# Two expert biases and a projection bias, moved from GpSimd to TensorE in the last layer of a four-layer kernel

## The chip, the cores and the metric

The kernel is one program on one core of a Trainium2 chip. The metric is the device time of one execution in microseconds. The engines are TensorE (PE; PEld is its weight load), VectorE (DVE), ScalarE (ACT), GpSimd (POOL) and SyncE (SP, which issues the transfers). The program of each engine is written out by hand, with semaphores between them.

## The reference

Four layers, each of the form x = x + attention(norm(x)) + ffn(norm(x)), on x of 8 batches, 512 tokens and 128 dimensions, all in f32. Only layer 3 is touched by the change:

```python
def _L3_attn_ref(x, Wq, bq, Wk, bk, Wv, bv, Wp, bp, bias_table, temperature):
    ...            # 16 heads of 8 dimensions, no causal mask, bias by distance
    att = jax.nn.softmax(energy / (scaling * temp), axis=-1)
    out = jnp.einsum('bhqk,bhkd->bhqd', att, v)
    out = out.transpose(0, 2, 1, 3).reshape(B, N, C)
    return out @ Wp + bp

def _L3_ffn_ref(x, Wr, br, W1, b1, W2, b2):
    k = 2
    scores0 = x[:, 0, :] @ Wr + br
    _, idx = jax.lax.top_k(scores0, k)            # two experts for each batch
    W1g, b1g = (W1[idx], b1[idx])
    W2g, b2g = (W2[idx], b2[idx])
    h = jnp.einsum('bsd,bkde->bkse', x, W1g) + b1g[:, :, None, :]
    h = jax.nn.gelu(h, approximate=False)
    o = jnp.einsum('bkse,bkef->bksf', h, W2g) + b2g[:, :, None, :]
    return jnp.sum(o, axis=1) / k
```

So a batch of layer 3 adds the same row of 128 numbers, (b2[e0] + b2[e1]) / 2 + bp, to each of its 512 tokens.

## The kernel before

x stays in SBUF for the whole program as [128, 32, 128] (token in a tile, tile, dimension); a batch is NT = 4 tiles. Layer 3 runs over the eight batches in a loop of pairs, with the last pair written out behind the loop. The heads of a batch are handled in four groups of four. Each group is first gone through for the row maxima ("max": PE's L501 with bias rows L505 to L510, DVE's L525), the maxima are turned into extra rows of Q (DVE L533 to L537, PE L550, DVE L558, a transfer at L483), and then gone through again for the exponentials ("score": PE's L572 with L576 and L579, ACT's L594) and the product with V ("attend": PE's L609, copied by DVE at L617). A list of steps fixes the order; each engine walks the same list and does its share of each step. While a group is in "score", the next group is in "max".

Beside the attention steps of the first group of a batch's successor, with six steps between one and the next, stands the tail of the batch: "hidden" (PE L2273, ACT L2243), "turn" (the division of the last group: PE L623, DVE L629 and L630), "mix" (PE L2281, DVE L2335), "turn_att" (PE L638, ACT L643) and "out" (PE L2289, DVE L2343). In the last batch the tail stands alone at the end. The start of the next batch ("center": DVE L359, L363, then POOL L387 and L389 for rstd, then DVE L371; "norm": PE L395; "k", "q", "v": PE L414 and L411; "choice": PE L2266, DVE L2322 to L2328) stands beside the scores of its predecessor's second group.

The steps of the tail share PSUM bank 1 in turns: `take` waits until the turn before has been emptied, `ready` until a named turn has been emptied, `there` until it has been filled. "aT" is the turn right before "out", and "h1" comes before "mix". "mix" multiplies the hidden values of the two experts by their second weights; DVE then makes acc = bank / 2 + x. "out" multiplies the turned attention by Wp; DVE writes x = bank + acc.

SP fetches the chosen experts' w1, w2, b1 and b2 in `pick`, eight transfers a batch, for the next batch once the last turn of the current one ("out") is filled. Before the change b2 lies in DRAM repeated 128 times, so that each of its transfers brings [128, 128], and bp is loaded once with a broadcast over the partitions. POOL's program for a batch is: rstd, the splitting of Q (L438 to L443), and then the bias work of L2223 to L2233, for which it waits for the experts. Four instructions make the constant row and add it to the batch's x in place. DVE waits for the count `bias_in` in "mix".

Two places in layers before it are of use for comparison: L2062 in layer 2 is a matmul with 32 rows of contraction, L2073 one with 64 columns of weights, and L2081 and L2083 alternate between 128 and 65 rows of contraction.

Of the kernel before, what the change touches and what calls it, by code (L numbers as in the profile page):

```python
# [7 lines left out]
ALU = mybir.AluOpType  # L8
# [127 lines left out]
def build(nc, a, out, layers=(0, 1, 2, 3)):  # L136

    stack = ExitStack()
    with stack:
# [211 lines left out]
        def settle(eng):  # L351


            eng.sem_inc(passed, 1)
# [477 lines left out]
        def load(sp, L, dst, src):  # L832
            sp.dma_start(dst, src).then_inc(L.weights, 16)
            L.loads += 1

        def pe_logits(pe, L, b, w, e):
            take(pe, L, b, "logit")
# [1302 lines left out]
        def layer3():  # L2140
# [8 lines left out]
            L.hankel = L.probs[:, 0:H * HANKEL // T, :].rearrange("p a (c i) -> p (a c) i", i=HANKEL)  # L2149
            L.table = carve([H, 384])  # L2150
            L.last = carve([H, 1])
            L.bp = carve([P, D])
            L.const = carve([P, D])
            L.wr, L.br = carve([P, E3]), carve([P, E3])
            L.sc, L.top, L.idx = carve([P, E3]), carve([P, 8]), carve([P, 8], U32)
            L.w1, L.w2 = carve([P, TOP3, D]), carve([P, TOP3, D])
            L.b1 = [carve([P, 1]) for _ in range(TOP3)]
            L.b2 = [carve([P, D]) for _ in range(TOP3)]
            L.hT = carve([P, TOP3, T])
            L.acc = carve([P, NT, D])  # L2160
            L.tabled = nc.dram_tensor("bias_by_distance", [H, 384], F32, kind="Internal").ap()
            L.chain = s("dve_chain", 19)
            L.chosen = s("experts_chosen", 1)
            L.picked = s("experts_in", 16 * 4 * TOP3, 1)
            L.bias_in = s("bias_added", 4)
            L.started += [L.picked]
            L.table_dve, L.table_dma = sem("table_dve"), sem("table_dma")
            L.bias_full, L.bias_free = sem("bias_full"), sem("bias_free")
# [13 lines left out]
            def sp_prog(sp):  # L2182
                L.loads = 0
                load(sp, L, L.table[:, 0:TABLE3], a["L3_attn_bias_table"])
                load(sp, L, L.scale, a["L3_attn_temperature"].partition_broadcast(P))
                for dst, name in ((L.w["k"], "L3_attn_Wk"), (L.w["q"], "L3_attn_Wq"), (L.w["v"], "L3_attn_Wv"),
                                  (L.w["o"], "L3_attn_Wp"), (L.bq, "L3_attn_bq"), (L.bk, "L3_attn_bk"),
                                  (L.wr, "L3_ffn_Wr")):
                    load(sp, L, dst, a[name])
                load(sp, L, L.bp, a["L3_attn_bp"].partition_broadcast(P))  # L2190
                load(sp, L, L.bv, a["L3_attn_bv"].partition_broadcast(P))
                load(sp, L, L.br, a["L3_ffn_br"].partition_broadcast(P))
                sp.wait_ge(L.table_dve, 3)
                sp.dma_start(L.tabled, L.table[:]).then_inc(L.table_dma, 16)
                sp.wait_ge(L.table_dma, 16)

                sp.dma_start(L.hankel[:], bass.AP(L.tabled.tensor, 0, [[1, P], [384, H], [1, HANKEL]])
                             ).then_inc(L.table_dma, 16)

                def pick(b):  # L2200
                    sp.wait_ge(L.late.full.sem, L.late.full.at(b, 0))
                    settle(sp)
                    sp.wait_ge(L.chosen.sem, L.chosen.at(b, 1))
                    settle(sp)
                    for k in range(TOP3):
                        e = sp.value_load(L.idx[0:1, k:k + 1], min_val=0, max_val=E3 - 1)
                        for dst, src in ((L.w1[:, k, :], a["L3_ffn_W1"][bass.ds(e, 1), :, :]),
                                         (L.w2[:, k, :], a["L3_ffn_W2"][bass.ds(e, 1), :, :]),
                                         (L.b1[k], a["L3_ffn_b1"][bass.ds(e, 1), :, :]),
                                         (L.b2[k], a["L3_ffn_b2"][bass.ds(e, 1), :, :])):  # L2210
                            sp.dma_start(dst, src.rearrange("e p c -> (e p) c")).then_inc(L.picked.sem, 16)
                sp_expand_ahead(sp, L, pick)

            def pool_prog(pool):
                pool_attention_setup(pool, L)

                def body(b):
                    pool_norm(pool, L, b)
                    pool_split_q(pool, L, b)
                    c = L.bias_in  # L2220
                    pool.wait_ge(L.picked.sem, L.picked.at(b, 16 * 4 * TOP3))
                    settle(pool)
                    pool.tensor_tensor(L.const[:], L.b2[0][:], L.b2[1][:], ALU.add).then_inc(c.sem, 1)  # L2223
                    pool.wait_ge(c.sem, c.at(b, 1))
                    settle(pool)
                    pool.tensor_scalar(L.const[:], L.const[:], 1.0 / TOP3, None, ALU.mult).then_inc(c.sem, 1)
                    pool.wait_ge(c.sem, c.at(b, 2))
                    settle(pool)
                    pool.tensor_tensor(L.const[:], L.const[:], L.bp[:], ALU.add).then_inc(c.sem, 1)
                    pool.wait_ge(c.sem, c.at(b, 3))  # L2230
                    settle(pool)
                    rows = x[:, bass.ds(b.index * NT, NT), :]
                    pool.tensor_tensor(rows, rows, L.const[:].unsqueeze(1).to_broadcast([P, NT, D]),  # L2233
                                       ALU.add).then_inc(c.sem, 1)
                each_batch(pool, body)

            def act_prog(act):
# [13 lines left out]
            def pe_prog(pe):  # L2251
                pe.wait_ge(L.weights, NW)
                pe.wait_ge(L.setup, 3 * L.copies)
                pe.wait_ge(L.padded, L.copies)

                pe.wait_ge(L.table_dma, 32)
                for n in range(H // 2):
                    if n >= 1:
                        pe.wait_ge(L.bias_free, n)
                    pe.matmul(bank[1][:], flip[:], L.hankel[:, 2 * n:2 * n + 2, :].rearrange("p h i -> p (h i)"),  # L2260
                              start=True, stop=True).then_inc(L.bias_full, 1)
                pe.wait_ge(L.bias_free, H // 2)

                def choice(pe, L, b, _):
                    bk = take(pe, L, b, "score")
                    fill(L, "score", pe.matmul(bk[:, 0:E3], xnT[b.parity][:, 0:1].to_broadcast([P, P]), L.wr[:],  # L2266
                                               start=True, stop=True))

                def hidden(pe, L, b, _):
                    pe.wait_ge(L.picked.sem, L.picked.at(b, 16 * 4 * TOP3))  # L2270
                    for k in range(TOP3):
                        bk = take(pe, L, b, f"h{k}")
                        fill(L, f"h{k}", pe.matmul(bk[:], L.w1[:, k, :], xnT[b.parity][:], start=True, stop=True))  # L2273

                def mix(pe, L, b, _):
                    take(pe, L, b, "mix")
                    ready(pe, L, b, f"h{TOP3 - 1}")
                    for t in range(NT):
                        cols = slice(t * P, (t + 1) * P)
                        for k in range(TOP3):  # L2280
                            ins = pe.matmul(bank[1][:, cols], L.hT[:, k, cols], L.w2[:, k, :], start=(k == 0),  # L2281
                                            stop=(k == TOP3 - 1))
                    fill(L, "mix", ins)

                def finish(pe, L, b, _):
                    take(pe, L, b, "out")
                    ready(pe, L, b, "aT")
                    for t in range(NT):
                        ins = pe.matmul(bank[1][:, t * P:(t + 1) * P], L.attT[:, t * P:(t + 1) * P], L.w["o"][:],  # L2289
                                        start=True, stop=True)  # L2290
                    fill(L, "out", ins)
                L.own_pe = {"choice": choice, "hidden": hidden, "mix": mix, "out": finish}

                def trip(b, more):
                    take_steps(pe_step, pe, L, b, more_steps if more else last_steps)
                pipelined(pe, L, lambda b: take_steps(pe_step, pe, L, b, first_steps), trip)

            def dve_prog(dve):
# [31 lines left out]
                def mix(dve, L, b, _):  # L2330
                    rows = x[:, bass.ds(b.index * NT, NT), :]
                    bk = there(dve, L, b, "mix")
                    dve.wait_ge(L.bias_in.sem, L.bias_in.at(b, 4))
                    settle(dve)
                    emptied(L, "mix", dve.scalar_tensor_tensor(  # L2335
                        out=L.acc[:], in0=bk[:].rearrange("p (t n) -> p t n", t=NT), scalar=1.0 / TOP3,
                        in1=rows, op0=ALU.mult, op1=ALU.add))
# [83 lines left out]
def _layouts(v):  # L2421
# [44 lines left out]
    out["L2_ffn_ba_up"] = v["L2_ffn_ba_up"].reshape(E2, 1, D)  # L2466
    for name in ("L3_attn_Wq", "L3_attn_Wk", "L3_attn_Wv", "L3_attn_Wp", "L3_ffn_Wr", "L3_ffn_W1", "L3_ffn_W2"):
        out[name] = by_dim(v[name]) if name in ("L3_attn_Wq", "L3_attn_Wk") else v[name]
    out["L3_attn_bp"] = v["L3_attn_bp"]
    out["L3_attn_bias_table"] = c(v["L3_attn_bias_table"].T)  # L2470
    out["L3_ffn_b1"] = v["L3_ffn_b1"].reshape(E3, D, 1)
    out["L3_ffn_b2"] = np.broadcast_to(v["L3_ffn_b2"][:, None, :], (E3, P, D))

    p, f = np.arange(P)[:, None], np.arange(P)[None, :]
    out["const_ident"] = np.eye(P, dtype=np.float32)
# [21 lines left out]
```

## Time and profile before

| what | value |
|---|---|
| median of three runs | 3440.54 us (3432.38 to 3443.14) |
| the profiled execution | 3443.14 us, span 3441.3 us |
| PE / PEld / DVE / ACT / POOL busy | 2630.3 / 1659.2 / 1621.3 / 1217.4 / 596.5 us |
| mean granted clock of TensorE | 0.874 of full |
| instructions on POOL | 600 |

The busy times are of the whole span. TensorE's busy time counts the modelled time of each matmul from start to end, which overlaps with that of the next; how long a matmul holds the engine is seen from the start of the next one. "Idle before" names, in brackets behind a row, how long the engine stood before this instruction and what it then went on for.

### The profile page before, as it was taken

What the parts mean: (1) busy time and instruction counts of PE and PEld (TensorE: products, weight loads), DVE (VectorE), ACT (ScalarE), POOL (GpSimd) and SP (SyncE); (2) the same over time, 40 slices, a digit from 0 to 9 for tenths busy, and PEclk for the clock granted to TensorE, in tenths of its full rate; (3) what the DMA queues carried; (4) which work ended last, traced back from release to release, by engine and by line L of the source; (5) the groups of instructions that cost most, each with busy time, mean ns of one, the idle gap of its engine ahead of it and who ended that gap; (6) DMA issues with size and microseconds to landing.
All of it is one profiled execution on the core that took longest, in us unless ns stands there. A gap on an engine that the chain in (4) does not pass through costs nothing. (4 is left out here: it accounts for less than half of the span.)

```text
span 3441.3 us, 52452 instructions
## 1 busy us (share of the span) xinstructions
PE 2630.3 (76%) x16466; PEld 1659.2 (48%) x16466; DVE 1621.3 (47%) x4013; ACT 1217.4 (35%) x2249; POOL 596.5 (17%) x600
## 2 busy tenths in 40 slices
PE   3677777799883778888887577777855888888887
PEld 1344444488771556656676244433423444444443
DVE  4556566400001444444433566666634555555563
ACT  0333333344433222222122244444421544444454
POOL 3322223000004433333102211111011000000000
PEclk7888889899995777778898699998977999999998
DMA  3111211266661000000054121111101111110111
GB/s 101 56 52 59 67 61 58 76 194 199 190 172 52 23 16 15 17 16 13 8 176 135 49 57 53 50 45 42 40 30 45 40 38 43 43 37 21 34 38 30
DMA packets 117031, 214.47 MB, mean 62 GB/s; under 512 B 20984, under 2 KB 89632, under 8 KB 109856
## 3 DMA queue, kind: packets, MB, share of 16 engines
q1 hardware_dynamic: 105088, 188.97, 18.3%
q0 software_dynamic: 10240, 20.99, 2.1%
q8 instruction: 143, 2.34, 0.3%
q10 hardware_dynamic: 1440, 1.18, 0.1%
q14 instruction: 120, 0.98, 0.1%
HBM read 158.50 MB, written 51.40 MB: 61 GB/s over the span
## 5 line engine op out<-in xcount | busy, mean ns | idle before, releaser
L525 DVE TENSOR_REDUCE arena<-bank 128x1 f32<-128x512 f32 (+3 forms) x1216 | 757.8, 658 | 207.2 <-PE bank L507 81.1
L501 PE MATMUL bank<-arena 125*128 125x512 bf16 (+3 forms) x1536 | 479.2, 349 | 165.9 <-DVE arena L525 91.8
L594 ACT ACTIVATE arena<-bank 128x512 f32<-128x512 f32 x640 | 370.5, 596 | 576.5 <-PE bank L584 563.2
L572 PE MATMUL bank<-arena 128*128 128x512 bf16 (+3 forms) x1536 | 461.3, 344 | 37.4 <-DMA arena<-arena 28.6
L594 ACT ACTIVATE arena<-bank,arena 128x512 f32<-128x512 f32 x512 | 339.3, 687 | 368.3 <-PE bank L572 208.5
L501 PEld LDWEIGHTS bank<-arena 125*128 125x128 bf16 x1536 | 143.6, 102 | 414.6 <-DVE arena L525 242.1
L609 PE MATMUL bank<-arena 128*32 128x512 f32 (+3 forms) x3072 | 329.9, 526 | 10.8 <-issue 6.3
L572 PEld LDWEIGHTS bank<-arena 128*128 128x128 bf16 x1536 | 140.1, 102 | 265.2 <-issue 139.7
L617 DVE COPY arena<-bank 128x512 f32<-128x512 f32 x96 | 66.4, 691 | 413.8 <-PE bank L609 398.3
L1854 DVE TENSOR_TENSOR arena<-bank,arena 128x512 f32<-128x512 f32 (+3 forms) x256 | 109.6, 482 | 199.5 <-PE bank L1720 193.7
L1098 PE MATMUL bank<-arena 128*128 128x128 f32 x1664 | 202.6, 275 | 0.1
L1245 ACT ACTIVATE arena<-bank,arena 128x256 f32<-128x256 f32 x320 | 131.9, 470 | 196.2 <-PE bank L1295 196.2
L1738 PEld LDWEIGHTS bank<-arena 128*128 128x128 f32 x1280 | 185.8, 232 | 22.3 <-issue 19.5
L1098 PEld LDWEIGHTS bank<-arena 128*128 128x128 f32 x1664 | 194.0, 192 | 0.5 <-ACT arena L1245 0.4
L1020 POOL DMA_INDIRECT back_rows<-sorted_out,back_now x160 | 154.0, 963 | 217.5 <-issue 155.1
L1738 PE MATMUL bank<-arena 128*128 128x65 f32 x1280 | 189.9, 316 | 1.0 <-DVE arena L1867 1.0
L1295 PE MATMUL bank<-arena 128*128 128x256 f32 x640 | 158.7, 391 | 38.1 <-DMA arena<-in_L_ffn_w 37.6
L1379 DVE TENSOR_TENSOR arena<-bank,arena 128x256 f32<-128x256 f32 x80 | 33.9, 424 | 322.4 <-PE bank L1098 322.4
L515 PE MATMUL bank<-mask_q,identb 128*128 128x128 bf16 (+2 forms) x704 | 183.5, 261 | 0.0
L1206 POOL DMA_INDIRECT sorted_in<-xn,arena x128 | 123.9, 968 | 333.4 <-PE bank L584 313.5
L584 PE MATMUL bank<-mask_k,identb 128*128 128x256 bf16 (+1 forms) x640 | 170.6, 267 | 0.0
L1720 PE MATMUL bank<-arena 64*128 64x128 f32 (+3 forms) x512 | 113.5, 554 | 55.3 <-DVE arena L1854 52.2
(249 smaller groups left out, 3702.5 us busy)
## 6 DMA issues: line engine op xcount, KB each, us to landing
arena<-in_L_ffn_w SPq DMA_DIRECT2D x80, 578.0 KB, 4.0
arena<-k_parts SPq DMA_DIRECT2D x48, 576.0 KB
arena<-q_parts SPq DMA_DIRECT2D x48, 576.0 KB
arena<-in_L_ffn_w SPq DMA_DIRECT2D x24, 768.0 KB, 4.5
arena<-sorted_in SPq DMA_DIRECT2D x104, 128.0 KB, 2.4
sorted_out<-arena SPq DMA_DIRECT2D x104, 128.0 KB, 4.0
k_parts<-arena SPq DMA_DIRECT2D x24, 384.0 KB
q_parts<-arena SPq DMA_DIRECT2D x72, 128.0 KB
```

What stands on the lines that cost most here:

```text
L501: ins = pe.matmul(mx[:, k * w:(k + 1) * w], Qx[0:KMAX, h, q * P:(q + 1) * P], Kx[0:KMAX, h, 0:w], start=(k == 0 or not L.causal), stop=not ...
L515: ins = pe.matmul(edge, identb[:], mask_q[:].unsqueeze(1).to_broadcast([P, n_heads, P]), start=False, stop=True, skip_group_check=True)
L525: dve.reduce_max(L.mx[:, g % 2, q, heads[0]:heads[-1] + 1], mx[:, 0:w * len(heads)].rearrange("p (j k) -> p j k", k=w), AX.X).then_inc(L.m ...
L572: ins = pe.matmul(st[:, c:c + w], Kx[:, h, kb * P:(kb + 1) * P], Qx[:, h, T - w:T], start=(c == 0), stop=not (L.causal or far), skip_group ...
L584: ins = pe.matmul(edge, identb[:], mask_k[:].unsqueeze(1).to_broadcast([P, len(at), P]), start=False, stop=True, skip_group_check=True)
L594: act.activation(L.probs[:, n % L.PR, 0:w], st[:, 0:w], ACT.Exp, scale=L.scale).then_inc(L.st_free.sem, 1)
L609: ins = pe.matmul(bank[2][j * VW:(j + 1) * VW, T - w:T], copy_of(L.Vx, b)[:, kb, g * HG + j, :], L.probs[:, (n + i) % L.PR, c:c + w], star ...
L1020: pool.indirect_dma_start(back_rows[:, t, k, :], None, L.ys, bass.IndirectOffsetOnAxis(L.back_now[b.parity][:, r:r + 1], 0)).then_inc(L.go ...
L1098: ins = pe.matmul(bank[2 + j % 2][:, h * D:(h + 1) * D], L.hT[j % 2][:, f, h * P:(h + 1) * P], down(j, f), start=(f == 0), stop=(f == 3))
L1245: act.activation(L.hT[j % 2][:, c, :], bank[4 + n % 4][:, c % 2 * BLK:(c % 2 + 1) * BLK], ACT.Gelu, bias=L.wbuf[j % 3][:, L.B1 + c:L.B1 + ...
L1295: ins = pe.matmul(bank[4 + n % 4][:, c % 2 * BLK:(c % 2 + 1) * BLK], L.wbuf[j % 3][:, L.W1 + c * P:L.W1 + (c + 1) * P], L.xT[j % 2][:], st ...
L1738: ins = pe.matmul(bk[:, t * V1W:(t + 1) * V1W], L.am[:, SLOTS * (h % 4) + slot, c:c + P], L.V[b.parity][:, kb, h, :], start=(kb == 0), sto ...
```

## The change

The constant row is no longer made and added by POOL. Instead PE adds the biases in PSUM: a matmul whose weights are one row of ones, [1, 128], and whose moving operand is the bias as one row adds the bias to all 128 tokens of a tile. `pe_bias` does this for a whole bank of four tiles at once, with the bias repeated four times by its access pattern (1 row by 512 columns). In "mix", the first expert's b2 is brought in this way, and the second's by four matmuls of 1 row by 128 columns, one ahead of each tile's two full matmuls. In "out", bp is brought in by `pe_bias` ahead of `pe_out`, which is a helper that the other layers use already. b2 and bp become [1, 128] in SBUF and are no longer repeated in DRAM. DVE's wait for `bias_in` in "mix" goes, as do the four POOL instructions of each batch.

```diff
+        def pe_bias(pe, bias):
+
+            return pe.matmul(bank[1][:], ones[0:1, :],
+                             bias[0:1, :].rearrange("p (o n) -> p o n", o=1).to_broadcast([1, NT, D]),
+                             start=True, stop=False, skip_group_check=True)
...
-            L.bp = carve([P, D])
-            L.const = carve([P, D])
+            L.bp = carve([1, D])
...
-            L.b2 = [carve([P, D]) for _ in range(TOP3)]
+            L.b2 = [carve([1, D]) for _ in range(TOP3)]
...
-            L.bias_in = s("bias_added", 4)
...
-                                  (L.wr, "L3_ffn_Wr")):
+                                  (L.bp, "L3_attn_bp"), (L.wr, "L3_ffn_Wr")):
                     load(sp, L, dst, a[name])
-                load(sp, L, L.bp, a["L3_attn_bp"].partition_broadcast(P))
...
                     pool_norm(pool, L, b)
                     pool_split_q(pool, L, b)
-                    c = L.bias_in
-                    pool.wait_ge(L.picked.sem, L.picked.at(b, 16 * 4 * TOP3))
-                    settle(pool)
-                    pool.tensor_tensor(L.const[:], L.b2[0][:], L.b2[1][:], ALU.add).then_inc(c.sem, 1)
...
-                    pool.tensor_scalar(L.const[:], L.const[:], 1.0 / TOP3, None, ALU.mult).then_inc(c.sem, 1)
...
-                    pool.tensor_tensor(L.const[:], L.const[:], L.bp[:], ALU.add).then_inc(c.sem, 1)
...
-                    pool.tensor_tensor(rows, rows, L.const[:].unsqueeze(1).to_broadcast([P, NT, D]),
-                                       ALU.add).then_inc(c.sem, 1)
...
                     take(pe, L, b, "mix")
                     ready(pe, L, b, f"h{TOP3 - 1}")
+                    pe_bias(pe, L.b2[0])
                     for t in range(NT):
                         cols = slice(t * P, (t + 1) * P)
+                        pe.matmul(bank[1][:, cols], ones[0:1, :], L.b2[1][:], start=False, stop=False,
+                                  skip_group_check=True)
                         for k in range(TOP3):
-                            ins = pe.matmul(bank[1][:, cols], L.hT[:, k, cols], L.w2[:, k, :], start=(k == 0),
-                                            stop=(k == TOP3 - 1))
+                            ins = pe.matmul(bank[1][:, cols], L.hT[:, k, cols], L.w2[:, k, :], start=False,
+                                            stop=(k == TOP3 - 1), skip_group_check=True)
...
                     take(pe, L, b, "out")
-                    ready(pe, L, b, "aT")
-                    for t in range(NT):
-                        ins = pe.matmul(bank[1][:, t * P:(t + 1) * P], L.attT[:, t * P:(t + 1) * P], L.w["o"][:],
-                                        start=True, stop=True)
-                    fill(L, "out", ins)
+                    pe_bias(pe, L.bp)
+                    fill(L, "out", pe_out(pe, L, b))
...
                     bk = there(dve, L, b, "mix")
-                    dve.wait_ge(L.bias_in.sem, L.bias_in.at(b, 4))
-                    settle(dve)
...
-    out["L3_ffn_b2"] = np.broadcast_to(v["L3_ffn_b2"][:, None, :], (E3, P, D))
+    out["L3_ffn_b2"] = v["L3_ffn_b2"].reshape(E3, 1, D)
```

## Rows read from the trace of the kernel before

**Rows 1.** Page, part 1: busy time, share, instructions; the row of PE.
```profile
PE 2630.3 (76%) x16466; PEld 1659.2 (48%) x16466; DVE 1621.3 (47%) x4013; ACT 1217.4 (35%) x2249; POOL 596.5 (17%) x600
```
**Rows 2.** Windows: span, then busy of PE, PEld, DVE, ACT, POOL, clock, DMA.
```profile
2732.00:2837.00 105.00, 87.83 (x516) 49.61 (x515) 59.65 (x123) 50.33 (x75) 6.91 (x9) 0.96 0.12 35
...
3362.00:3441.00 79.00, 59.63 (x336) 29.72 (x328) 29.27 (x56) 34.93 (x52) 2.68 (x4) 0.89 0.10 27
```
**Rows 3.** Timeline around "mix" of one batch: start us, length us, instruction.
```profile
2736.96 1.95 PE L2281 MATMUL bank<-arena 128*128 128x128 f32 x16
...
2738.74 0.38 PE L501 MATMUL bank<-arena 125*128 125x512 bf16 x1
...
2738.96 0.38 PE L572 MATMUL bank<-arena 128*128 128x512 bf16 x1
...
2739.26 0.69 DVE L2335 SCALAR_TENSOR_TENSOR arena<-bank,x 128x512 f32<-128x512 f32 x1 [1.61 <-PE bank L2281]
...
2740.61 0.39 PE L501 MATMUL bank<-arena 125*128 125x512 bf16 x1 [0.83 <-DVE arena L525]
```
**Rows 4.** Timeline around "out" of the same batch.
```profile
2744.79 1.06 PE L2289 MATMUL bank<-arena 128*128 128x128 f32 x8
...
2745.69 0.38 PE L501 MATMUL bank<-arena 125*128 125x512 bf16 x1
...
2745.89 0.69 DVE L2343 TENSOR_TENSOR x<-bank,arena 128x512 f32 x1 [0.72 <-PE bank L2289]
...
2748.31 0.33 PE L550 MATMUL bank<-identb,arena 128*12 128x128 bf16 x3 [1.80 <-DVE arena L537]
```
**Rows 5.** Timeline in layer 2: into 32 rows and out again.
```profile
2317.75 0.22 PE L515 MATMUL bank<-mask_q,identb 128*128 128x128 bf16 x1
...
2317.90 1.13 PE L2062 MATMUL bank<-arena 32*128 32x512 f32 x4
...
2318.96 0.39 PE L501 MATMUL bank<-arena 125*128 125x512 bf16 x1
```
**Rows 6.** Timeline in layer 2: 65 rows, first and last of four.
```profile
2339.60 0.39 PE L2083 MATMUL bank<-arena 65*128 65x128 f32 x2
...
2340.94 0.39 PE L2083 MATMUL bank<-arena 65*128 65x128 f32 x2
```
**Rows 7.** Timeline in layer 2: 64 columns of weights and what follows.
```profile
2332.20 1.07 PE L2073 MATMUL bank<-xnT,arena 128*64 128x512 f32 x2
...
2333.21 0.39 PE L501 MATMUL bank<-arena 125*128 125x256 bf16 x2
```
**Rows 8.** Timeline in layer 3: one full f32 matmul and what follows.
```profile
2765.11 1.02 PE L414 MATMUL bank<-xnT,arena 128*128 128x512 f32 x2
...
2765.97 0.38 PE L501 MATMUL bank<-arena 125*128 125x512 bf16 x1
```
**Rows 9.** Timeline behind rows 4: 12 columns beside 32 columns.
```profile
2748.43 0.63 PE L609 MATMUL bank<-arena 128*32 128x512 f32 x3
2748.48 0.22 PE L550 MATMUL bank<-identb,arena 128*12 128x128 bf16 x1
```
**Rows 10.** Timeline at the norm of two batches, POOL and DVE.
```profile
2755.61 1.27 POOL L2233 TENSOR_TENSOR x<-x,arena 128x512 f32 x1 [0.29 <-POOL arena L2229]
...
2756.96 0.23 POOL L387 TENSOR_SCALAR rstd<-mean_var 128x4 f32<-128x4 f32 x1
...
2758.51 1.11 DVE L371 TENSOR_SCALAR xn<-x,mean_var,rstd 128x128 f32 x4 [2.02 <-POOL rstd L389]
...
2861.20 0.23 POOL L387 TENSOR_SCALAR rstd<-mean_var 128x4 f32<-128x4 f32 x1 [2.54 <-DVE mean_var L363]
```
**Rows 11.** Timeline of the tail of the last batch.
```profile
3425.22 2.05 PE L2281 MATMUL bank<-arena 128*128 128x128 f32 x16 [0.68 <-DVE arena L630]
...
3427.46 0.69 DVE L2335 SCALAR_TENSOR_TENSOR arena<-bank,x 128x512 f32<-128x512 f32 x1 [2.30 <-PE bank L2281]
...
3429.63 1.74 PE L2289 MATMUL bank<-arena 128*128 128x128 f32 x8 [0.77 <-ACT arena L643]
```

More of the change, by code:

```diff
@@ L2219, in body @@
                     pool_split_q(pool, L, b)
-                    c = L.bias_in
-                    pool.wait_ge(L.picked.sem, L.picked.at(b, 16 * 4 * TOP3))
-                    settle(pool)
-                    pool.tensor_tensor(L.const[:], L.b2[0][:], L.b2[1][:], ALU.add).then_inc(c.sem, 1)
-                    pool.wait_ge(c.sem, c.at(b, 1))
-                    settle(pool)
-                    pool.tensor_scalar(L.const[:], L.const[:], 1.0 / TOP3, None, ALU.mult).then_inc(c.sem, 1)
-                    pool.wait_ge(c.sem, c.at(b, 2))
-                    settle(pool)
-                    pool.tensor_tensor(L.const[:], L.const[:], L.bp[:], ALU.add).then_inc(c.sem, 1)
-                    pool.wait_ge(c.sem, c.at(b, 3))
-                    settle(pool)
-                    rows = x[:, bass.ds(b.index * NT, NT), :]
-                    pool.tensor_tensor(rows, rows, L.const[:].unsqueeze(1).to_broadcast([P, NT, D]),
-                                       ALU.add).then_inc(c.sem, 1)
                 each_batch(pool, body)
@@ L2468, in _layouts @@
         out[name] = by_dim(v[name]) if name in ("L3_attn_Wq", "L3_attn_Wk") else v[name]
-    out["L3_attn_bp"] = v["L3_attn_bp"]
+    out["L3_attn_bp"] = v["L3_attn_bp"].reshape(1, D)
     out["L3_attn_bias_table"] = c(v["L3_attn_bias_table"].T)
     out["L3_ffn_b1"] = v["L3_ffn_b1"].reshape(E3, D, 1)
-    out["L3_ffn_b2"] = np.broadcast_to(v["L3_ffn_b2"][:, None, :], (E3, P, D))
+    out["L3_ffn_b2"] = v["L3_ffn_b2"].reshape(E3, 1, D)
     p, f = np.arange(P)[:, None], np.arange(P)[None, :]
```

## The prediction

> **What bounds the kernel now.** I read the page first: PE is the busiest engine of the whole span [rows 1]. The change touches layer 3 alone (the last quarter of the span), so I then read the stretches of one batch each. In one of 105 us, PE is busy 87.83 us, DVE 59.65, ACT 50.33 and POOL 6.91; the last stretch, where nothing runs ahead for a next batch, looks alike [rows 2]. The reader is to see that POOL has a hundred microseconds of room in a batch and PE very little. Third, the timeline around the two places that the change makes longer on PE. At "mix", PE goes straight from its 16 records to the next L501, DVE stands waiting 1.61 us for "mix" and starts L2335 behind it, and a later L501 of PE waits in turn for DVE [rows 3]. At "out", PE goes straight on to L501, DVE waits 0.72 us for the result, and PE later waits 1.80 us at L550 for the chain on DVE that began behind it [rows 4]. So each of the two sits on a path PE, DVE, PE without slack: what is added there moves everything behind it. Last, the timeline at the norm of the following batch, where POOL's rstd is awaited by DVE, and PE behind DVE [rows 10].
>
> **What the change adds on PE, per batch.** An f32 matmul appears as two records.
> 1. Two bias matmuls with 512 columns (one in "mix", one in "out"). The nearest row is L414, full shape: its two records start at 2765.11 and the next matmul at 2765.97, so 0.86 us [rows 8]. Twice that is 1.72 us.
> 2. Four matmuls of one row by 128 columns with the second expert's bias. In "mix" eight matmuls of 128 columns hold PE from 2736.96 to 2738.74, 0.22 us each [rows 3]. Four are 0.89 us.
> That a matmul of one row costs as much as one of 128 is taken from L2083: 65 rows alternate with 128 rows, and four alternations are spaced (2340.94 - 2339.60) / 3 = 0.447 us a pair, 0.223 us a matmul, the same 0.22 [rows 6]. Together 2.61 us a batch, 20.9 us over eight.
> 3. What a change of the array's shape costs. With 65 rows there is none [rows 6]. With 32 rows there is: L515 with 128 bf16 columns starts at 2317.75 and L2062 only 0.15 us later, where 128 columns take some 0.05 (a quarter of the 0.22 us by which bf16 matmuls of 512 columns follow one another in the timeline, as from 2738.74 on), so about 0.10 us to enter. Its four records, equal in time to one full 0.86 us, hold the next L501 back until 2318.96, 1.06 us, so 0.20 us to leave [rows 5]. L2073 with 64 columns holds the next L501 back for 2333.21 - 2332.20 = 1.01 us, so 0.15 us to leave [rows 7]. Is one row treated as 32 rows are? No row shows a one-row matmul. The nearest is L550 with 12 columns: its last record starts at 2748.48, after records of L609 with 32 columns have begun at 2748.43, so 12 columns share the shape of 32 instead of being drained from it [rows 9]. A small number is thus rounded up to 32, and I take one row as 32 rows, at L2062's 0.30 us for a pair of in and out. The bounds are 0 (as for 65 rows) and 0.30 with a third on top for weight loads that can no longer be loaded ahead of so short a matmul, 0.40; the value lies nearest to L2062, which is small in rows and not in columns. In "mix" the order is bias, then for each of four row blocks one one-row and two full matmuls; the first bias and the first small one are neighbours, so four pairs; "out" has one. Five pairs are 1.5 us a batch, 12.0 us over eight (0 to 16).
>
> The Trainium skill, TensorEngine Tiling (Array Packing), Key Properties, says that changing the tiling mode drains TensorE, and gives no figure; this trace agrees for 32 rows and for 64 columns, with the 0.30 us and the 0.15 us worked out above from [rows 5, 7]. The Trainium skill, TensorE: Matmul & The Clock Gate, in the table under "Why this matters for your kernels", says that a single matmul with K=32 takes the same time as with K=128; by that sentence alone the sum would lack the 12.0 us and be rival B.
>
> 4. In the last batch PE is slower in "out": 1.74 us for L2289 against 1.06, so most of it ran at the lower of the clock's two levels [rows 4, 11]. Its bias of 512 columns, at half the rate, is 0.86 us dearer: 0.9 us once.
>
> **What it removes.** DVE at L2335 first waits for "mix", then for the bias count, then starts: 0.35 us from the modelled end of PE's records (2738.91) to 2739.26 in the loop [rows 3], 0.19 us in the last batch [rows 11]. At "out", with one wait fewer, it is 0.04 us (2744.79 + 1.06 to 2745.89) [rows 4]. I save 0.15 to 0.31 us a batch, 1.2 to 2.5 us, and take 1.7. POOL loses four instructions a batch. Only L2233 ever stands in the way: in rows 10 L387 starts at 2756.96, right behind it (2755.61 + 1.27), and DVE's L371 waits for it. Had it been free, L387 could have begun a few tenths earlier; in the batch after, it started at 2861.20 with POOL idle since 2858.66, where nothing is won [rows 10]. I take 0.3 us over the kernel, bounds 0 and 2.5 (all 1.27 us twice). The other three POOL instructions cost nothing now, covered by POOL's idle time, and give nothing back. The loads of b2 shrink from 64 to 0.5 KB and bp likewise, but SP issues as many as before, behind the same waits, and the experts' weights are used a batch later; bp is moved one place up in a queue of twelve, all awaited together. Both at zero. L2335, L2343 and all DVE work stay as they are. `take("out")` already waits for "aT" to be emptied (same bank, earlier turn), so the bias of "out" can't be slipped into that wait.
>
> **Sum.** 20.9 + 12.0 + 0.9 - 1.7 - 0.3 = +31.8 us. The profiled execution took 3443.14 us (its span of 3441.3 and 1.8 around it), so the changed one would take 3474.9. That execution is 2.6 us above the median of the runs, 3440.54; on the median it is 3472.3, which I predict as 3472 (+0.9%).
>
> **Rivals.**
> A, the above: 3472.
> B, one row drains nothing: 12.0 us less, 3460. For it: L2083 with 65 rows alternates for free. Against: L2062.
> C, PE's additions are swallowed by waits it has anyway, such as the 1.80 us at L550 [rows 4]. If four fifths of the 33.8 us were, 6.8 - 2.0 = 4.8 us remain, 3445, which is within 0.3% (about 10 us, what this kernel's measurement can tell from no change). Against: that wait hangs on DVE's chain, which itself waits for "out".
> D, the other side: POOL and the bias wait were the late ones. This needs DVE's start at "mix" and rstd to be held by POOL, 0.35 us x 8 plus 1.27 us x 8 = 13 us, and the PE additions hidden as in C entirely: 3428. It decides once under 3 us of PE's 33.8 stay in the open, as faster by over 0.3% needs 10 of the 13. Against: POOL ended L2233 at 2756.88, most of a batch ahead of the "mix" that counts on it, and in the batch after it was idle for 2.54 us before L387, where it holds nothing [rows 10].
> E, leaving a one-row matmul costs more, or the clock falls more often in the stretches after "mix". With 0.6 us a pair it is 24 us instead of 12: 3484.
>
> **How the numbers follow.** A 0.62, B 0.17, E 0.08, C 0.08, D 0.05. The likeliest gives 3472. The range: 3455 to 3485; it takes in A with its bounds (drain 0 to 0.40, the savings), B and nearly E, and leaves out C and D and a little of E. Faster by over 0.3% is D, 0.05; within 0.3% is C, 0.08; slower is A, B and E, 0.87.
>
> **What the changed profile would show.** The f32 records of one row at some 0.86 us for 512 columns a pair and 0.22 for 128; in "mix" a stretch from its first record to the next L501 of 1.8 + 1.75 + 1.2 = 4.7 us instead of 1.8, and in "out" 2.1 instead of 0.9 [rows 3, 4]; DVE idle before the mix instruction 1.6 + 2.9 - 0.2 = 4.3 us; a period of a batch in layer 3 longer by some 4 us, layers 0 to 2 unchanged; L387 waiting for DVE in every batch. B is right if "mix" is 3.5 us long. The prediction is wrong if "mix" is as long as said and the batch doesn't grow with it (C), or if PE's clock in layer 3 differs from before.

## The result, and the profile after

The changed kernel takes 3499.84 us (median of four runs, 3492.54 to 3501.68), beside 3441.84 us for the kernel before: ratio 1.0157, 95% interval 1.0125 to 1.0190. Two further sets of runs of the same kernel, below, gave 1.0145 and 1.0138. It is slower, as forecast, but by 48 to 58 us (the medians of the three sets) where 31.8 were summed up, and outside the range, which ended at 3485.

The two lines below are from the page of the profile after: its span, and the busy time of each engine. This execution took 3477.37 us, 34.2 us more than the profiled one of before and 15 us less than the fastest of the four runs above. That it is close to the sum is luck: in it layer 3 was 43 us longer, and its layers 0 to 2, whose code is unchanged, ended 9 us earlier than in the profile before.

```profile
span 3475.6 us, 52384 instructions
PE 2654.8 (76%) x16428; PEld 1674.8 (48%) x16562; DVE 1621.6 (47%) x4013; ACT 1217.7 (35%) x2249; POOL 574.6 (17%) x568
```

Beside [rows 1] PE is 24.5 us busier and POOL 21.9 us less; DVE and ACT are the same. To see only layer 3, I take it from its first rstd (L387) to the end of the span, 2582.86 to 3441.3 before and 2573.89 to 3475.6 after: 858.4 and 901.7 us. The windows of the trace after show that stretch, and then "mix" of four batches. Behind the bounds stand the length, the busy time of PE, PEld, DVE, ACT and POOL, the granted clock as a share of full speed, and the DMA's share and rate.

```profile
2574.00:3475.60 901.60, 725.07 (x4010) 402.04 (x4080) 461.46 (x944) 387.28 (x575) 33.37 (x40) 0.93 0.11 34
```
```profile
2726.20:2733.10 6.90, 6.90 (x28) 4.97 (x28) 0.65 (x2) 0.79 (x2) 0.00 (x0) 0.73 0.02 4
3047.90:3053.00 5.10, 5.10 (x28) 3.69 (x28) 0.66 (x2) 0.81 (x2) 0.00 (x0) 1.00 0.00 0
3155.80:3161.90 6.10, 6.10 (x28) 4.50 (x28) 0.59 (x1) 0.74 (x2) 0.00 (x0) 0.79 0.02 4
3262.70:3269.70 7.00, 7.00 (x28) 5.18 (x28) 0.61 (x2) 0.75 (x2) 0.00 (x0) 0.68 0.00 0
```

The same 28 records (the 26 of "mix" and two beside them) take 5.1 us in one batch and 7.0 in another, and the clock column says why: 1.00 against 0.68. A share between 0.5 and 1 is a mean of the two levels, 1.2 and 2.4 GHz. The timeline of the batch at full clock, PE alone, from the record ahead of "mix" to DVE's instruction:

```profile
3047.65 0.38 PE L572 MATMUL bank<-arena 128*128 128x512 bf16 x1
...
3047.96 1.12 PE L838 MATMUL bank<-arena,ones 1*128 1x512 f32 x2
...
3048.93 0.38 PE L2269 MATMUL bank<-arena,ones 1*128 1x128 f32 x2
...
3049.23 0.71 PE L2272 MATMUL bank<-arena 128*128 128x128 f32 x4
...
3049.88 0.48 PE L2269 MATMUL bank<-arena,ones 1*128 1x128 f32 x2
...
3050.29 0.71 PE L2272 MATMUL bank<-arena 128*128 128x128 f32 x4
...
3052.40 0.71 PE L2272 MATMUL bank<-arena 128*128 128x128 f32 x4
...
3052.95 0.82 PE L501 MATMUL bank<-arena 125*128 125x512 bf16 x2
...
3053.15 0.69 DVE L2321 SCALAR_TENSOR_TENSOR arena<-bank,x 128x512 f32<-128x512 f32 x1 [4.59 <-PE bank L2272]
```

From L838 to the next L501 "mix" is 4.99 us long, where it was 1.78 [rows 3]. Behind the first L2269, whose neighbour L838 has its shape, L2272 and L2269 alternate every 0.65 and 0.41 us. DVE starts 0.04 us after the modelled end of PE's last record (3052.40 + 0.71), no longer 0.35. In the batch at 2726.20 the first alternation looks the same, and then everything stretches:

```profile
2728.16 0.48 PE L2269 MATMUL bank<-arena,ones 1*128 1x128 f32 x2
...
2729.88 1.22 PE L2272 MATMUL bank<-arena 128*128 128x128 f32 x4
...
2731.03 0.79 PE L2269 MATMUL bank<-arena,ones 1*128 1x128 f32 x2
...
2733.14 0.69 DVE L2321 SCALAR_TENSOR_TENSOR arena<-bank,x 128x512 f32<-128x512 f32 x1 [6.29 <-PE bank L2272]
```

The windows of this batch place the fall: at the lower level from 2729.3 to 2736.1, and at full clock ahead of it and behind it.

```profile
2726.00:2729.30 3.30, 3.30 (x17) 2.08 (x15) 0.85 (x2) 0.99 (x2) 0.00 (x0) 1.00 0.03 7
2729.30:2736.10 6.80, 6.58 (x20) 4.19 (x22) 2.84 (x5) 1.37 (x2) 0.00 (x0) 0.50 0.00 0
2736.10:2740.00 3.90, 3.90 (x24) 1.80 (x22) 1.68 (x3) 2.55 (x4) 0.00 (x0) 1.00 0.00 0
```

The next lines show "out" in the same batch, and rstd of the next batch:

```profile
2738.95 0.38 PE L576 MATMUL bank<-arena,ident 128*128 128x128 f32 x2
...
2739.27 1.12 PE L838 MATMUL bank<-arena,ones 1*128 1x512 f32 x2
...
2740.32 1.16 PE L649 MATMUL bank<-arena 128*128 128x128 f32 x8
...
2741.31 0.38 PE L501 MATMUL bank<-arena 125*128 125x512 bf16 x1
...
2743.93 0.33 PE L550 MATMUL bank<-identb,arena 128*12 128x128 bf16 x3 [1.80 <-DVE arena L537]
...
2752.39 0.23 POOL L387 TENSOR_SCALAR rstd<-mean_var 128x4 f32<-128x4 f32 x1 [93.71 <-DVE mean_var L363]
```

From L838 to L501 it is 2.04 us instead of 0.90 [rows 4]; from the L576 ahead of it to L501 it is 2.36 us, where the kernel before took 1.12, from this line to 2745.69:

```profile
2744.57 0.38 PE L576 MATMUL bank<-arena,ident 128*128 128x128 f32 x2
```

PE's wait at L550 is 1.80 us, as before to the hundredth: nothing of what was added has been absorbed there. POOL now waits for DVE at every norm. In the loop the period of a batch grew from 101.7 us (L387 at 2655.01 to L387 at 3265.11, six batches) to 107.0 (2646.51 to 3288.62), where some 4 us were forecast.

### The profile page after: what moved, and what is told of

Its sections match the earlier page's. It is cut to its first block and busy times, and to the rows that moved or that the text cites. A ratio compares the mean times of both kernels' runs of the same rounds, so it can differ in the third digit from the quotient of the medians.

```text
span 3475.6 us, 52384 instructions
## 1 busy us (share of the span) xinstructions
PE 2654.8 (76%) x16428; PEld 1674.8 (48%) x16562; DVE 1621.6 (47%) x4013; ACT 1217.7 (35%) x2249; POOL 574.6 (17%) x568
## 3 DMA queue, kind: packets, MB, share of 16 engines
q8 instruction: 144, 2.36, 0.3%
## 5 line engine op out<-in xcount | busy, mean ns | idle before, releaser
L501 PE MATMUL bank<-arena 125*128 125x512 bf16 (+3 forms) x1536 | 482.4, 351 | 172.4 <-DVE arena L525 83.1
L572 PE MATMUL bank<-arena 128*128 128x512 bf16 (+3 forms) x1402 | 406.9, 338 | 10.8 <-ACT arena L594 5.3
L501 PEld LDWEIGHTS bank<-arena 125*128 125x128 bf16 x1536 | 143.5, 102 | 410.2 <-DVE arena L525 237.6
L387 POOL TENSOR_SCALAR rstd<-mean_var 128x4 f32<-128x4 f32 x32 | 7.4, 230 | 1129.0 <-DVE mean_var L363 983.6
L515 PE MATMUL bank<-mask_q,identb 128*128 128x128 bf16 (+2 forms) x704 | 183.6, 261 | 0.0
```

Of the source, the lines that this page charges most:

```text
L501: ins = pe.matmul(mx[:, k * w:(k + 1) * w], Qx[0:KMAX, h, q * P:(q + 1) * P], Kx[0:KMAX, h, 0:w], start=(k == 0 or not L.causal), stop=not ...
L515: ins = pe.matmul(edge, identb[:], mask_q[:].unsqueeze(1).to_broadcast([P, n_heads, P]), start=False, stop=True, skip_group_check=True)
L572: ins = pe.matmul(st[:, c:c + w], Kx[:, h, kb * P:(kb + 1) * P], Qx[:, h, T - w:T], start=(c == 0), stop=not (L.causal or far), skip_group ...
```

## The experiments

The theory after this result: columns, shape changes and a lower clock each have a price. The rivals: the extra time lies elsewhere, or the matmuls with fewer rows are dear in themselves. "Mix" is read from the first record of it to the next L501. In seven of the eight batches other work follows behind it; these are called the loop batches here.

**The changed kernel again.** The same kernel, run once more.

> The changed kernel once more, for the spread of its runs and a second profile. Its median was 58 us above the kernel before, its profiled execution only 34 us above, although layer 3 alone had grown by 43 us in it. Theory: the added matmuls and the drains are the same in every execution, 33 to 36 us, and what varies is TensorE's clock, which fell to the lower level during 'mix' in most batches of the profile. Then an execution near 3500 us shows the same count and order of instructions in 'mix', and more or longer stretches at the lower clock than one near 3477. Rival: the extra time of the slower executions lies in layers 0 to 2 and has nothing to do with the change; then layer 3 is 43 us longer in every profile.

3490.10 us, ratio 1.0145 (1.0119 to 1.0172). Its profiled execution took 3494.11 us. Layer 3 was 906.3 us long, 48 us more than before, and had begun 3 us later than in the profile before instead of 9 us earlier. So both the theory and the rival had a part in the difference between the two profiles: 12 us of it lay in layers 0 to 2, with no change of code, and 5 us in layer 3, where "mix" again was 4.99 us long once and 5.9 to 7.1 us in the six other loop batches.

**128 rows.**

The weights of every bias matmul become 128 rows of ones. The bias stands in row 0 of its operand, with zeros below it.

```diff
+ROWS = 128
...
-            return pe.matmul(bank[1][:], ones[0:1, :],
+            return pe.matmul(bank[1][:], ones[0:ROWS, :],
...
-                        pe.matmul(bank[1][:, cols], ones[0:1, :], L.b2[1][:], start=False, stop=False,
+                        pe.matmul(bank[1][:, cols], ones[0:ROWS, :], L.b2[1][:], start=False, stop=False,
...
-    out["L3_ffn_b2"] = v["L3_ffn_b2"].reshape(E3, 1, D)
+    out["L3_ffn_b2"] = np.pad(v["L3_ffn_b2"].reshape(E3, 1, D), ((0, 0), (0, ROWS - 1), (0, 0)))
```

> All bias matmuls with 128 rows of ones; the bias stands in row 0 and zeros in rows 1 to 127. Same columns, same count of instructions. Theory (change of shape, and the clock that falls with it): no drains, so 'mix' takes 1.8 + 1.75 = 3.5 us and 'out' 2.0 us, the clock stays up in 'mix', and the time is 2.6 us x 8 - 2 = 19 us above the kernel before, ratio 1.0055 (1.004 to 1.007). Rival (the columns and the accumulation cost more than I charged, whatever the rows): as the change, 1.0157. Second rival (drains yes, clock no): 1.0055 in time but the granted clock in 'mix' falls as with one row.

3463.36 us, ratio 1.0071 (1.0052 to 1.0091). "Mix" was 3.53 us in each of the seven, with no fall of the clock. The ratio is just above what was expected (1.004 to 1.007), and half of the loss of the change is gone with the same columns and instructions.

**One change of shape in "mix".** Both biases come ahead of the full matmuls.

```diff
                     pe_bias(pe, L.b2[0])
+                    pe_bias(pe, L.b2[1], False)
                     for t in range(NT):
                         cols = slice(t * P, (t + 1) * P)
-                        pe.matmul(bank[1][:, cols], ones[0:1, :], L.b2[1][:], start=False, stop=False,
-                                  skip_group_check=True)
```

> In 'mix' both experts' biases are brought in one after the other over the whole bank (two matmuls of 1 row by 512 columns) ahead of the eight full matmuls, so the shape changes once instead of four times. Same columns. Theory (each pair of shape changes costs 0.385 us as measured in the profile after): 3 pairs less, 1.15 us a batch, 9 us in all, and where the clock no longer falls in 'mix' up to 15 us more: 35 to 49 us above the kernel before, 1.010 to 1.014. Rival (one row is what lowers the clock, not the alternation): 1.013 to 1.014 with the low stretches still there. Rival (shape changes cost nothing): 1.0157.

3478.90 us, ratio 1.0118 (1.0096 to 1.0139), 11 us under the changed kernel beside it, in the middle of what was expected. PE's timeline in one batch:

```profile
2843.97 1.98 PE L838 MATMUL bank<-arena,ones 1*128 1x512 f32 x4
2845.88 2.96 PE L2271 MATMUL bank<-arena 128*128 128x128 f32 x16
2848.64 0.63 PE L501 MATMUL bank<-arena 125*128 125x512 bf16 x1
```

The sixteen full records take 2.76 us here, where they took 1.78 at full clock before [rows 3]; "mix" varied from 3.80 to 5.25 us, and the clock fell in six of the seven. In the one batch where it stayed up, "mix" took 3.80 us, 1.19 less than 4.99, for three pairs of changes fewer. So fewer changes save their price, as the theory had it, but its hope that the clock would stay up failed: the sign of the rival that one row lowers the clock is there (low for 3.4 us at a time, where it was 6.8 in the changed kernel).

**Without the biases.** POOL's work and the wait stay removed, the bias matmuls too; b2 and bp are left out of the output.

> The change without any of its bias matmuls, so that the two experts' b2 and bp are left out of the output; POOL's four instructions and VectorE's wait for them stay removed. Theory: what is removed was worth 0.2 to 0.3 us a batch, so 1.5 to 3 us, ratio 0.9992 to 0.9996, the same within what can be measured. Rival: POOL's work held the norm or 'mix' by more, 10 to 13 us, ratio 0.996 to 0.997; then the matmuls cost that much more than the difference of the two kernels.

3434.77 us, ratio 0.9991 (0.9976 to 1.0007). What was removed was worth 3.0 us by the medians, which can't be told from nothing; the interval allows up to 8 us, and the rival with 10 us or more lies outside it.

**65 rows and 32 rows.** As for 128 rows, with the slice and the padding at 65 and at 32.

> The bias matmuls with 65 rows of ones (bias in row 0, zeros in 64 rows). With 128 rows 'mix' took 3.53 us and the clock never fell in it; with one row 4.98 us at full clock, and the clock fell in most batches. Theory A (the drain at a change of shape is what is charged, and the idle time of TensorE in the drains is what lowers the clock): as with 128 rows, 'mix' 3.53 us, no low clock in it, ratio 1.006 to 1.008. Theory B (drains for the time, but few active rows lower the clock): 'mix' 3.53 us long at full clock, with stretches at the lower clock in it in some batches, and a ratio between 1.007 and 1.011. Rival (every matmul under 128 rows costs more): 'mix' near 5 us.

> The bias matmuls with 32 rows, as L2062 in layer 2 has them. I took one row to be treated as 32 rows are. If that holds, 'mix' has the spacing that one row gives, 4.98 us at full clock and 0.31 us from the record before. In the clock theory A (drains) tells of no difference from one row: ratio 1.0145 to 1.0157. Theory B (active rows) allows fewer or shorter low stretches with 32 rows than with one: ratio 1.010 to 1.014. Rival (one row is a case of its own, dearer than 32): 'mix' at 4.2 us, from the 0.30 us a pair of L2062 in the profile of before.

65 rows: 3461.45 us, ratio 1.0060 (1.0039 to 1.0082). 32 rows: 3474.19 us, 1.0100 (1.0073 to 1.0126). First PE's timeline with 65 rows:

```profile
2727.63 1.02 PE L839 MATMUL bank<-arena,ones 65*128 65x512 f32 x2
2728.49 0.38 PE L2270 MATMUL bank<-arena,ones 65*128 65x128 f32 x2
2728.71 0.61 PE L2273 MATMUL bank<-arena 128*128 128x128 f32 x4
2729.16 0.39 PE L2270 MATMUL bank<-arena,ones 65*128 65x128 f32 x2
2729.38 0.61 PE L2273 MATMUL bank<-arena 128*128 128x128 f32 x4
...
2731.17 0.38 PE L502 MATMUL bank<-arena 125*128 125x512 bf16 x1
```

and with 32 rows:

```profile
2726.61 0.38 PE L573 MATMUL bank<-arena 128*128 128x512 bf16 x1
2726.92 1.12 PE L839 MATMUL bank<-arena,ones 32*128 32x512 f32 x2
2727.88 0.38 PE L2270 MATMUL bank<-arena,ones 32*128 32x128 f32 x2
2728.19 0.71 PE L2273 MATMUL bank<-arena 128*128 128x128 f32 x4
2728.84 0.48 PE L2270 MATMUL bank<-arena,ones 32*128 32x128 f32 x2
2729.25 0.71 PE L2273 MATMUL bank<-arena 128*128 128x128 f32 x4
...
2731.91 0.38 PE L502 MATMUL bank<-arena 125*128 125x512 bf16 x1
```

65 rows alternate every 0.22 and 0.45 us, without a gap, and "mix" is 3.54 us, at full clock in all seven. With 32 rows it is 4.99 us, and each spacing equals that of one row above to 0.01 us. So one row is treated as 32 rows are, and the shape costs 0.20 + 0.19 = 0.39 us a pair. The rival by L2062's 0.30 falls.

The weight loads (PEld) show where a change spends its time. First those of the batch at full clock with one row, then those with 65 rows:

```profile
3047.96 0.29 PEld L838 LDWEIGHTS bank<-arena,ones 1*128 1x128 f32 x2 [0.36 <-issue]
3048.50 0.18 PEld L2269 LDWEIGHTS bank<-arena,ones 1*128 1x128 f32 x1 [0.24 <-issue]
3049.23 0.52 PEld L2272 LDWEIGHTS bank<-arena 128*128 128x128 f32 x4
```
```profile
2728.07 0.19 PEld L2270 LDWEIGHTS bank<-arena,ones 65*128 65x128 f32 x1 [0.24 <-issue]
2728.60 0.53 PEld L2273 LDWEIGHTS bank<-arena 128*128 128x128 f32 x4
```

With 65 rows L2273's load starts 0.11 us ahead of its matmul (2728.71), beside the matmul before it. With one row L838's and L2272's loads start together with their matmuls (3047.96 and 3049.23). A change thus costs in two halves: about 0.09 us ahead of the first record of the new shape, and 0.10 us between its first record and its second. At L838 the second half is seen by the load for L2269 (L2270 with 65 rows), which starts with L838's second record: 0.54 us behind the first with one row, 0.44 with 65; from there to the bias matmul of 128 columns it is 0.43 and 0.42 us.

What differs between 32 rows and one is the clock, here in the windows over "mix" of three batches with 32 rows:

```profile
2726.90:2731.90 5.00, 5.00 (x27) 3.64 (x27) 0.62 (x2) 0.77 (x2) 0.00 (x0) 1.00 0.02 5
2831.60:2836.60 5.00, 5.00 (x28) 3.66 (x28) 0.55 (x1) 0.70 (x2) 0.00 (x0) 1.00 0.00 0
2937.40:2942.40 5.00, 5.00 (x28) 3.65 (x28) 0.55 (x1) 0.70 (x2) 0.00 (x0) 1.00 0.02 5
```

It fell in one of the seven loop batches, against six of seven with one row. The theory that the gaps at the changes lower the clock (1.0145 to 1.0157 for 32 rows) falls with this; the one by active rows (1.010 to 1.014) stands.

**Only "out".** The kernel before, with bp alone moved to PE.

```diff
-                    pool.tensor_tensor(L.const[:], L.const[:], L.bp[:], ALU.add).then_inc(c.sem, 1)
...
                     take(pe, L, b, "out")
+                    pe_bias(pe, L.bp)
+                    fill(L, "out", pe_out(pe, L, b))
```

> Only the change in 'out': bp is brought in by TensorE with one row by 512 columns; POOL still makes the mean of the two b2 and adds it to x, and VectorE waits for it in 'mix'. Theory: 'out' is longer by 1.24 us, of that 0.09 to enter; 8 batches make 10 us, plus a little for the last batch at the lower clock; 'mix' stays at 1.78 us with no low clock in it. Ratio 1.003 to 1.004. Then the other 38 to 48 us of the change are those of 'mix'. Rival (the 1.80 us wait at L550 swallows it): no difference, ratio 1.000.

3450.28 us, ratio 1.0035 (1.0018 to 1.0053). "Mix" kept its 1.78 us and full clock. The wait at L550 swallows nothing. Of the changed kernel's loss some four fifths are "mix".

**All three biases in one matmul, 128 rows and 4 rows.** One tile holds both b2 in rows 0 and 1 and bp in rows 2 and 3; DVE halves the sum, so bp comes in once.

```diff
-            L.bp = carve([1, D])
+            L.b4 = carve([ROWS, D])
...
-            L.b2 = [carve([1, D]) for _ in range(TOP3)]
+            L.b2 = [L.b4[k:k + 1, :] for k in range(TOP3)]
...
-                    pe_bias(pe, L.b2[0])
+                    pe_bias(pe, L.b4)
```

> All three biases in one matmul in 'mix': rows 0 and 1 of one tile are the two b2, rows 2 and 3 are bp twice (VectorE halves the sum), rows 4 to 127 are zeros; weights are 128 rows of ones. 'out' is as before the change. Theory: 512 columns at 0.86 us a batch, no drain, no low clock in 'mix', and the 0.3 to 0.4 us a batch that the removal of POOL's work gives: 6.9 - 3 = +4 us, ratio 1.001, no difference from the kernel before that can be told. Rival (any work added in 'mix' brings the clock down): ratio 1.004 or more, with low stretches in 'mix'.

> All three biases in one matmul of 4 rows by 512 columns in 'mix' (rows: both b2, and bp twice), 'out' as before the change. One pair of shape changes a batch and 0.86 us with few rows. With 128 rows this was 1.0003. Theory: 'mix' takes 1.78 + 0.86 + 0.39 = 3.0 us and comes 0.09 us later; (0.86 + 0.39 + 0.09) x 8 = 10.7, less the 3 us of what is removed: +8 us, ratio 1.002, if the clock stays up, as it did at 'out' with a single bias matmul. Rival (any matmul with few rows lowers the clock in 'mix'): ratio 1.006, with low stretches in 'mix'.

128 rows: 3445.20 us, ratio 1.0003 (0.9986 to 1.0021), "mix" 2.64 us. 4 rows: 3450.16 us, 1.0027 (1.0008 to 1.0046). PE's timeline with 4 rows:

```profile
2835.83 1.12 PE L839 MATMUL bank<-arena,ones 4*128 4x512 f32 x2
2836.88 2.05 PE L2270 MATMUL bank<-arena 128*128 128x128 f32 x16
2838.77 0.82 PE L502 MATMUL bank<-arena 125*128 125x512 bf16 x2
```

"Mix" takes 2.94 us and the clock stays up in all seven. Both came as the theory had it. This is the way to do the change: with 128 rows it frees POOL and costs nothing that can be told from no change. No version beats the kernel before, and by the run without biases none of this kind could by more than 3 us or so (8 at the end of its interval).

**One row and 32 rows side by side.** The same two kernels, run once more.

> The changed kernel beside the one with 32 rows on one chip, five rounds. The two have the same instructions with the same spacing at full clock (4.98 and 4.99 us in 'mix'), so a difference between them can only come from the clock. Theory (few active rows lower the clock): this one is 15 to 20 us above the kernel with 32 rows, ratio 1.014 to 1.016 to the kernel before, with the clock low in 'mix' in most of the seven loop batches of the profile. Rival (the earlier difference between them was chance of the runs): the two agree within 5 us.

> 32 rows of ones once more, beside the changed kernel. Theory: ratio 1.009 to 1.011, the clock low in 'mix' in at most two of the seven loop batches. Rival: as the changed kernel, 1.0145 or more.

One row 3488.89 us, ratio 1.0138 (1.0112 to 1.0165); 32 rows 3478.47 us, 1.0124 (1.0097 to 1.0152). The medians are 10.4 us apart, less than the 15 to 20 that I expected, the ratios only 0.0014 (5 us), and their intervals overlap; 32 rows came out above the 1.009 to 1.011 as well. The traces are clearer than the times. Over the three profiles of the one-row kernel the clock stayed up in "mix" in 4 of 21 loop batches, over the two with 32 rows in 13 of 14. Layer 3 was 901.7, 906.3 and 906.2 us long with one row, 896.4 and 896.6 with 32. That difference lies in "mix" itself: summed over the seven loop batches, its length beyond 4.99 us each was 8.4, 8.7 and 7.9 us with one row, and 1.3 and 0 with 32.

## Why the prediction was wrong

Point by point, in its own order.

- **What bounds the kernel**: right. At "mix" and "out" nothing was absorbed (the 1.80 us at L550 are unchanged, DVE's idle time before "mix" grew from 1.61 to 4.59 us at full clock, against 4.3 forecast).
- **Columns, 20.9 us**: right. "Mix" went from 1.78 to 3.53 us with 128 rows (1.75, forecast 1.75); layer 3 was 852.6 us without biases and 873.9 with 128 rows, 21.3 us. A single profile can be some 5 us off: with 65 rows, of the same spacing, layer 3 was 878.5 us. By the medians (128 and 65 rows 26 and 22 us above the kernel before, without biases 3 below) the columns cost 25 to 29 us, with intervals that still take in 20.9.
- **One row is as 32 rows**: right, shown by equal spacing. The row it was inferred from, L550, is small in columns and not in rows, so this was a lucky guess as much as a reading.
- **Shape changes, 12.0 us**: right in kind, too small. In "mix" they cost 4.99 - 3.54 = 1.45 us and 0.09 us ahead of it; "out" went from 1.12 us between L576 and L501 to 2.36 us (2738.95 to 2741.31), 1.24 more, of which 0.86 is the bias and 0.38 the shape. 1.92 us a batch, 15.4 over eight. I took L2062's 0.30 us for a pair; between short f32 matmuls it is 0.39. The 0.20 us that I called leaving held the second half of entering (the records after L2062's first come at 2318.43, 0.53 us behind it, where 65 rows give 0.44), and what follows L2062 is a bf16 matmul of one record, which has no second half to pay: L515 comes 0.22 us behind that L501 (2319.18), as bf16 matmuls of 512 columns do elsewhere. All of mine are followed by f32 matmuls. The Trainium skill, TensorE: Matmul & The Clock Gate, Part 3, "The mechanism", says that weight loads overlap running matmuls only where their row groups differ or a background buffer is used. The overlap is what the loads with 65 rows show (0.11 us ahead of their matmul), and at a change of shape it is missing; which of the two conditions fails there, no run here isolates.
- **The clock, 0.9 us once**: this is the step that failed, an effect priced for one "out" only, where the runs showed 8 to 10 us in the loop and some 3 in the last batch. I priced the lower clock for the last "out" alone and gave the loop batches none, though the clock already fell in this layer (0.94 over layer 3 before). In the profile before, all its 15 falls there came behind stretches with gaps, PE busy at most 2.0 us of the 3 us ahead of the fall. The falls in "mix" are of another kind: ahead of all 17, PE's records, as the profile models them, fill 2.9 to 3.0 us of the 3. A look at PE's idle time alone would not have found them. A clock in layer 3 that differs from before was the prediction's own sign of being wrong, and it came: 0.93 against 0.94, and 0.68 to 1.00 in the "mix" of the loop where it was 1.00 in all eight batches before. With one row it fell during "mix" in 17 of 21 loop batches, and then for about 6.8 us, past the end of "mix". With the same instructions and spacing, 32 rows keep it up. The difference between them is what one row costs through the clock in the loop: 896.5 against a mean of 904.7 us in layer 3, 8.2 us, of which 7.7 lie within "mix"; the medians side by side gave 10.4, the ratios 5. I take 8 to 10 us. The last batch pays with one row and with 32 alike. Its stretch behind L387 grew from 176.2 us (3265.11 to 3441.3) to 187.0, 189.7 and 188.9 us with one row (190.4 and 188.4 with 32), of which two batches of added work at full clock explain some 9; that leaves some 3 us, for the lower clock took part or all of the last "mix" too (it took 7.0 to 9.5 us to the next L638, 2.99 before), not "out" alone.
- **What is removed, 2.0 us**: right (3.0 us by the medians, not distinguishable from 0; layer 3 was 5.8 us shorter in the one profile).
- **Rivals**: B fell with "mix" at 4.99 us, not 3.5; C and D with the unchanged waits and with the run without biases. E had named both what was missing, dearer shape changes and a clock that falls after "mix", at a chance of 0.08 and as the one or the other, not both. Its 3484 was nearest.

Summed up again, with what the runs showed: 20.9 + 15.4 + 8 to 10 (clock in the loop) + 3 (last batch) - 3 = +44 to +46 us, against 43 to 48 us in layer 3 in the three profiles. The medians of the three sets lie 48 to 58 us above the kernel before. The remaining few microseconds aren't located. Layers 0 to 2, the same code in all, ended up to 22 us apart in the three profiles of the changed kernel (first L387 at 2573.9 to 2595.7), which is enough for it, though it isn't shown to be the cause. Why the clock falls with one row and stays up with 32 is open too.

## What to carry to other kernels

A bias brought in by a matmul costs its columns whatever its rows. Where a row or a few alternate with full matmuls, each pair of changes costs 0.39 us more here, and a burst of them can take the clock down for work that follows, so pad the operand with zeros to 65 rows or more, or gather all small-row work in one matmul. Padding to 32 keeps the clock up but not the 0.39 us; nothing between 33 and 64 rows was tried. Before moving work off an engine that is idle nine tenths of the time, ask what that engine held up: here some 3 us.

A price for PE work is read at the clock that will hold during it: look at where in the trace the clock falls already, and put a term in the sum for the new stretch falling too.

## What the runs showed of the hardware that I had not expected

- Rows of contraction matter for the granted clock, not only gaps: the same records with the same spacing kept full clock with 32 rows (31 of them ones times zeros) in 13 of 14 loop batches and with one row in 4 of 21. With 65 and 128 rows, without gaps, it never fell in "mix" in the loop.
- Once fallen, the clock took the matmuls after "mix" with it: in the batch at 2726.20 it was down until 2736.1, while "mix" ended at 2732.8.
- A single matmul of 4 rows by 512 columns in "mix" (fold4), or of one row by 512 columns in "out" (out_only), left the clock up there in all seven loop batches.
- A change of shape also delays the second f32 record of the new shape (0.10 us), so its price depends on what follows: 0.20 us into f32 matmuls, 0.10 into a bf16 one.
- Layers 0 to 2, unchanged, took from 9 us less to 13 us more than in the profile of before in the three profiles of the changed kernel (13 us less with only "out" changed), so that a single profiled execution can agree with a sum by chance.
